# Making the 24 later value tiles between the residual MLP jobs, and spreading the gathers over the query/key jobs

## The chip, the cores and the metric

The kernel runs on one core of one Trainium2 chip, in one launch. The metric is device microseconds of one execution, the median of several runs. All data that passes between the stages lives in SBUF, PSUM or internal DRAM tensors of the core.

## The reference

Two transformer-like layers on x of 4 x 1024 x 128 (float32). Only layer 0 bears on the change:

```python
xn = layernorm(x)                                  # 4096 rows of 128
s  = attn(xn)     # 16 heads of 64: q, k, v = xn @ qkv_w.T; rope on q and k; softmax(q k / 8 + distance bias) v; @ out_w.T
a  = layer_norm(xn) * attn_nw + attn_nb
# top-1 of 8 experts, capacity 512 each, rows in order; a row beyond the capacity gets nothing from its expert
moe = combine(expert_mlp(dispatch(a)))             # 128 -> 512 -> 128, gelu
res = gelu(a @ res_inter_w + b) @ res_output_w + b # residual MLP
g  = silu(res * coef[:, :1] + moe * coef[:, 1:] + xn)
x  = x + s * g
```

Layer 1 follows (a recurrence and an MLP with LoRA experts); the change does not touch it.

## The kernel before

The program is a row of blocks. Every engine runs its own instruction list in a block, ordered by hand, and the engines meet only at semaphores; all of them meet at the end of a block. The blocks are `prepare`, `experts`, `project`, `attend`, `recur` and `finish`. In `prepare` and `experts` all loops are unrolled; the 64 jobs of `project` and the 64 head units of `attend` run in hardware loops (`Fori`).

`prepare` (0 to 168 us of the span) loads x, normalizes it, transposes it to `xn_t` and `a_t`, and computes the routing logits. The rows are 32 tiles of 128 rows. The value projection of one tile, `xn_t` (128 columns) times `wv` (128 x 1024), is two halves of 512 columns. Each half is one float32 matmul into PSUM (recorded as two passes), a ScalarE copy to bfloat16 (the high part), a subtraction PSUM minus high part (the low part), and each finished tile is written to DRAM (`vscr`, 512 KB) for the attention. The first 8 tiles (NV) are made here, between the transposes (L317 to L326, L381 to L390). The routing then goes as a long chain of small VectorE operations (L272 to L313) with one visit to TensorE for counts (L375, L376, at `COUNT_JOB = 1`). Its last result is `scatter_idx`, on which GpSimd waits to issue 32 indirect scatters, one for each tile, of the rows of A into `dispatch` (L235).

Beside this chain TensorE and ScalarE run the residual MLP in 8 jobs of 512 rows: `hidden(j)`, four matmuls of 128x512 (L351), a gelu of each on ScalarE (L410) into one of two buffers, `out(j)`, 16 matmuls of 128x128 (L363), and a copy of the result into G0 (L161). TensorE's order is `hidden(j+1)`, then `out(j)`.

`experts` (169 to 238 us) runs the 8 expert MLPs and makes the rope tables. `project` (238 to 552 us) first makes the other 24 value tiles, in the same way, in 8 PSUM half slots and four SBUF buffers, with SP issuing the writes (L701). Meanwhile GpSimd issues 32 indirect gathers of expert rows (L720), waits for all, multiplies them by the combine weight (L724) and adds them to G0 (L726) in two operations over the whole 128 x 4096 array; ScalarE then applies silu to G0 (L764). Only then do the query/key jobs start, 64 of them (8 head pairs of 8 chunks of 512 rows). A job is four float32 matmuls (L798), three VectorE operations on 128x1024 for rope (L665, L666, L670), a ScalarE copy to bfloat16 (L678), a GpSimd subtraction for the low part (L684), and a write of 512 KB from ScalarE's queue (L689). Two PSUM buffers, two to four SBUF buffers in a ring; VectorE may be three jobs ahead of GpSimd (`lo_ready`), and the write trails the copy by two jobs (`LEAD`).

Of the kernel before, what the change touches and what calls it, by code (L numbers as in the profile page):

```python
# [100 lines left out]
def prepare(nc, K, io, sb, ps, sem):  # L101
# [31 lines left out]
    lps, counts = ps("logit_ps", [P, NT, E + 2]), ps("count_ps", [P, 2, NT, E])  # L133
# [8 lines left out]
    va_wr = [sem(f"va_wr{s}") for s in range(2)]  # L142

# [10 lines left out]
    COUNT_JOB = 1  # L154

    def hidden_ps(i):
        return tp[i // 2][:, i % 2 * CH:i % 2 * CH + CH]
# [9 lines left out]
    with nc.Block() as block:  # L167
# [72 lines left out]
        def _(v):  # L240
# [31 lines left out]
            ch.link(v.tensor_copy(lg[:], lps[:]))  # L272
# [40 lines left out]
            v.tensor_copy(scatter_idx[:], col[:, 11, :]).then_inc(idx_ready, 1)  # L313

        @block.tensor
        def _(pe):
            def v_rows(t):  # L317

                pe.wait_ge(K.wv_in, DMA)
                pe.wait_ge(tr_out, 2 * (t // BT) + 1)  # L320
                for c in range(2):
                    if t >= 1:
                        pe.wait_ge(va_taken, 2 * t + c - 1)
                    pe.matmul(op[c][:].rearrange("p t d -> p (t d)"), K.XNT[:, t * P:t * P + P],
                              K.wv[:, c * CH:c * CH + CH], start=True, stop=True).then_inc(va_ready, 1)
# [21 lines left out]
            def hidden(j):  # L347
                for i in range(FT):
                    if j >= 1:
                        pe.wait_ge(h_out, FT * (j - 1) + i + 1)  # L350
                    pe.matmul(hidden_ps(i), w1r[:, i * P:i * P + P], AT[:, j * CH:j * CH + CH],  # L351
                              start=True, stop=True).then_inc(h_ready, 1)

            def out(j):
                s = j % 2
                if j >= 2:
                    pe.wait_ge(o_out, j - 1)
                else:
                    pe.wait_ge(va_taken, 2 * NV)
                for i in range(FT):  # L360
                    pe.wait_ge(h_out, FT * j + i + 1)
                    for c in range(CT):
                        mm = pe.matmul(op[s][:, c, :], hT[s][:, i, c * P:c * P + P], w2r[:, i, :],  # L363
                                       start=(i == 0 and c == 0), stop=(i == FT - 1), skip_group_check=True)
                mm.then_inc(o_ready, 1)

            hidden(0)
            for j in range(NR):
                if j + 1 < NR:
                    hidden(j + 1)  # L370
# [6 lines left out]
                out(j)  # L377

        @block.scalar
        def _(act):  # L380
# [23 lines left out]
            act.wait_ge(va_lo, 2 * NV)  # L404
            for j in range(NR):
                for i in range(FT):
                    act.wait_ge(h_ready, FT * j + i + 1)
                    if j >= 2 and i == 0:
                        act.wait_ge(o_ready, j - 1)
                    act.activation(hT[j % 2][:, i, :], hidden_ps(i), ACT.Gelu_apprx_tanh,  # L410
                                   bias=b1r[:, i:i + 1]).then_inc(h_out, 1)
                if j >= 1:
                    take_out(act, j - 1)
            take_out(act, NR - 1)
# [13 lines left out]
def experts(nc, K, io, sb, ps, sem):  # L428
# [30 lines left out]
    with nc.Block() as block:  # L459

        @block.sync
        def _(sp):
# [3 lines left out]
            for i in range(P // (DH // 2)):  # L466
                sp.dma_start(freq[32 * i:32 * i + 32, :], io["freqs"].rearrange("(p o) -> p o", o=1)).then_inc(fr_in, DMA)
            sp.dma_start(bp[:], io["bias_p"]).then_inc(bp_in, DMA)
# [151 lines left out]
def project(nc, K, io, sb, ps, sem):  # L620

    v_ready, vhi, vlo, v_wr = sem("v_ready"), sem("vhi"), sem("vlo"), [sem(f"v_wr{s}") for s in range(4)]
    wqk_in = [sem("wqk_in0"), sem("wqk_in1")]
# [5 lines left out]
    wv = K.wv  # L629
    NW = NT - NV  # L630
    vt = [sb(f"v_parts{i}", [P, H, 2, DH], BF16) for i in range(4)]
    wqk = [sb(f"wqk{i}", [P, 4, P]) for i in range(2)]
# [59 lines left out]
    with nc.Block() as block:  # L692

        @block.sync
        def _(sp):
            for r in range(2):
                sp.dma_start(wqk[r][:], io["wqk"][r]).then_inc(wqk_in[r], DMA)
            for t in range(NW):
                sp.wait_ge(vhi, 2 * t + 2)
                sp.wait_ge(vlo, 2 * t + 2)  # L700
                sp.dma_start(K.vscr[NV + t], vt[t % 4][:].rearrange("p h a d -> p h (a d)")).then_inc(v_wr[t % 4], DMA)  # L701
            for s in range(4):
                sp.wait_ge(v_wr[s], DMA * NW // 4)
# [12 lines left out]
        @block.gpsimd  # L716
        def _(g):

            for t in range(NT):
# [12 lines left out]
        @block.vector  # L732
        def _(v):
            for t in range(NW):
                for c in range(2):
                    n = 2 * t + c
                    v.wait_ge(vhi, n + 1)
                    hs = slice(c * H // 2, c * H // 2 + H // 2)
                    v.tensor_tensor(vt[t % 4][:, hs, 1, :],
                                    pp[n // 4 % 2][:, n % 4, :].rearrange("p (h d) -> p h d", d=DH),  # L740
                                    vt[t % 4][:, hs, 0, :], ALU.subtract).then_inc(vlo, 1)

            v.wait_ge(vlo, 2 * NW)
# [9 lines left out]
        def _(act):  # L753
            for t in range(NW):
                if t >= 4:
                    act.wait_ge(v_wr[t % 4], DMA * (t // 4))
                for c in range(2):
                    n = 2 * t + c
                    act.wait_ge(v_ready, n + 1)
                    act.copy(vt[t % 4][:, c * H // 2:c * H // 2 + H // 2, 0, :],  # L760
                             pp[n // 4 % 2][:, n % 4, :].rearrange("p (h d) -> p h d", d=DH)).then_inc(vhi, 1)

            act.wait_ge(mix_ready, 1)
            act.activation(K.G0[:], K.G0[:], ACT.Silu).then_inc(g0_ready, 1)  # L764

# [9 lines left out]
            run_jobs(act, step)  # L775
            for s in range(4):
                act.wait_ge(qk_wr[s], G * (DMA * NJ // 4) + 1)

        @block.tensor
        def _(pe):  # L780
            for t in range(NW):
                for c in range(2):
                    n = 2 * t + c
                    if n >= 8:
                        pe.wait_ge(vlo, n - 7)
                    pe.matmul(pp[n // 4 % 2][:, n % 4, :], XNT[:, (NV + t) * P:(NV + t + 1) * P], wv[:, c * CH:c * CH + CH],
                              start=True, stop=True).then_inc(v_ready, 1)
# [795 lines left out]
def program(nc, io):  # L1583

    with ExitStack() as outer:
# [27 lines left out]
        with ExitStack() as heads:  # L1613
# [5 lines left out]
            with ExitStack() as layer0:  # L1619
                sb0, _ = maker(layer0)  # L1620
                K.XNT = sb0("xn_t", [P, B * S])
                K.wv, K.wv_in = sb0("wv", [P, H * DH]), sem("wv_in")
                K.COS, K.SIN = sb0("cos_tables", [P, 2, S]), sb0("sin_tables", [P, 2, S])
# [72 lines left out]
```

## Time and profile before

| | us |
|---|---|
| median of 3 runs (2015.58 to 2019.97) | 2019.54 |
| the profiled execution, its own time | 2019.78 |
| its span, first to last instruction | 2018.0 |
| busy: TensorE, VectorE, GpSimd, ScalarE | 1810.2, 1517.4, 1470.0, 1149.4 |
| mean granted TensorE clock, share of full speed | 0.956 |

The span is read from the first to the last instruction of the core; 1.8 us of the profiled execution's time lie around it. An engine's busy time over the whole span is an average over blocks with different limits, so the change has to be judged block by block. The page's chain of work that ended last reaches back only over some 3% of the span, inside the last block, and does not reach the blocks of the change.

### The profile page before, as it was taken

The numbers are of one execution on the slowest core, as the hardware profiler recorded it, in microseconds if no ns is written. First come the engines' busy times: TensorE is split into PE (matmuls) and PEld (weight loads), VectorE is DVE, ScalarE is ACT, GpSimd is POOL, SyncE is SP. The second block draws the span as 40 slices with busy tenths as digits, with TensorE's granted clock in tenths as the row PEclk, the third lists the DMA queues.
The fourth block names the chain that finished last, engine by engine and source line by source line (L and its number), as shares of the span: only waits on it lengthen the run. The fifth ranks groups of instructions, "written<-read, shape, count | busy, mean of one in ns | idle before, by whom it ended". The sixth has DMA issues, their size and how long they took to land. (4 is left out here: it accounts for less than half of the span.)

```text
span 2018.0 us, 39811 instructions
## 1 busy us (share of the span) xinstructions
PE 1810.2 (90%) x12166; PEld 1052.0 (52%) x12356; DVE 1517.4 (75%) x2940; ACT 1149.4 (57%) x1691; POOL 1470.0 (73%) x865
## 2 busy tenths in 40 slices
PE   3959879999779999999999989999999999599978
PEld 2636523333245555555555555555555555356656
DVE  8303548999888888878878888878888888698841
ACT  3413533222267777777777767777777777322123
POOL 4260274555579999989989899899899899655521
PEclk8779979999989999999999999999999999799989
DMA  4212483446569888888888888888888888500001
GB/s 138 94 42 62 127 203 128 151 146 210 167 135 180 185 194 178 193 185 180 193 180 183 186 177 184 188 182 182 187 183 184 197 184 184 135 1 1 1 6 37
DMA packets 714150, 295.28 MB, mean 146 GB/s; under 512 B 619264, under 2 KB 678658, under 8 KB 714064
## 3 DMA queue, kind: packets, MB, share of 16 engines
q1 hardware_dynamic: 678240, 257.81, 56.5%
q10 hardware_dynamic: 33792, 33.56, 4.9%
q0 software_dynamic: 2048, 3.15, 1.2%
q8 instruction: 23, 0.38, 0.1%
q14 instruction: 47, 0.39, 0.1%
HBM read 102.39 MB, written 58.85 MB: 80 GB/s over the span
## 5 line engine op out<-in xcount | busy, mean ns | idle before, releaser
L1134 POOL TENSOR_TENSOR probs_lo<-probs 128x1024 bf16<-128x1024 f32 x512 | 957.1, 1901 | 78.9 <-DMA probs_t_lo<-probs_lo 51.3
L1102 ACT ACTIVATE probs<-scores,neg_max 128x1024 f32<-128x1024 f32 x512 | 588.6, 1150 | 264.0 <-DVE neg_max L1028 232.6
L1028 DVE CUSTOM_DVE_ANT_0 scores<-score_ps,bias_tab 128x1024 f32<-128x1024 f32 x512 | 624.8, 1221 | 116.9 <-issue 111.6
L952 PE MATMUL score_ps<-k_lo_lo,q_hi_lo 128*128 128x512 bf16 x1024 | 392.8, 384 | 35.8 <-DVE ident_bf L1088 15.6
L960 PEld LDWEIGHTS turn_ps<-ident_bf,probs 128*128 128x128 bf16 x4096 | 273.2, 98 | 144.6 <-issue 25.3
L960 PE MATMUL turn_ps<-ident_bf,probs 128*128 128x128 bf16 x4096 | 314.9, 220 | 18.9 <-ACT probs L1102 18.8
L951 PE MATMUL score_ps<-k_hi_hi,q_hi_lo 128*128 128x512 bf16 x834 | 321.4, 385 | 2.1 <-DMA k_lo_lo<-qk_parts 2.1
L979 PE MATMUL pv_ps<-probs_t_hi,v_hi_lo 128*128 128x512 bf16 x1024 | 262.9, 380 | 10.4 <-DVE share L1068 7.0
L1109 ACT COPY probs_t_hi<-turn_ps 128x1024 bf16<-128x1024 bf16 x256 | 255.9, 1000 | 21.2 <-PE turn_ps L960 17.3
L798 PE MATMUL proj_ps<-xn_t,wqk 128*128 128x512 f32 x512 | 231.1, 604 | 7.2 <-DVE rotated L670 5.8
L684 POOL TENSOR_TENSOR qk_parts<-rotated,qk_parts 128x1024 bf16<-128x1024 f32 x64 | 136.3, 2132 | 111.0 <-ACT qk_parts L678 110.8
L951 PEld LDWEIGHTS score_ps<-k_hi_hi,q_hi_lo 128*128 128x128 bf16 x1024 | 100.8, 98 | 168.8 <-DVE neg_max L1028 44.5
L1050 DVE COPY probs_t_hi<-turn_ps 128x1024 bf16<-128x1024 bf16 x256 | 175.6, 686 | 0.0
L1142 POOL TENSOR_TENSOR s<-s,share 128x512 f32 (+1 forms) x128 | 163.7, 1279 | 6.9 <-DVE share L1068 6.9
L798 PEld LDWEIGHTS proj_ps<-xn_t,wqk 128*128 128x128 f32 x512 | 92.1, 189 | 146.3 <-issue 92.3
L678 ACT CAST qk_parts<-rotated 128x1024 bf16<-128x1024 f32 x64 | 66.9, 1046 | 170.6 <-DVE rotated L670 161.7
L952 PEld LDWEIGHTS score_ps<-k_lo_lo,q_hi_lo 128*128 128x128 bf16 x1024 | 101.2, 99 | 92.0 <-issue 3.0
L1350 POOL TENSOR_TENSOR q_state<-state,q_t 128x1024 f32<-128x1024 f32 x32 | 76.5, 2391 | 81.8 <-DVE state L1294 72.5
L984 PE MATMUL pv_ps<-probs_t_lo,v_hi_lo 128*64 128x512 bf16 x1024 | 134.7, 385 | 0.0
L979 PEld LDWEIGHTS pv_ps<-probs_t_hi,v_hi_lo 128*128 128x128 bf16 x1024 | 87.4, 98 | 81.1 <-DVE share L1068 19.5
L1102 ACT ACTIVATION_READ_ACCUMULATOR probs<-scores,neg_max 128x1 f32 x512 | 96.1, 188 | 0.0
L997 PE MATMUL pv_ps<-wo_parts,out_t_hi 128*128 (+1 forms) x512 | 92.7, 224 | 2.8 <-DVE out_t_lo L1058 2.8
(213 smaller groups left out, 2392.6 us busy)
## 6 DMA issues: line engine op xcount, KB each, us to landing
qk_parts<-qk_parts ACTq DMA_DIRECT2D x64, 512.0 KB, 3.2
q_hi_lo<-qk_parts SPq DMA_DIRECT2D x128, 128.0 KB, 2.8
k_hi_hi<-qk_parts SPq DMA_DIRECT2D x128, 128.0 KB, 2.9
k_lo_lo<-qk_parts SPq DMA_DIRECT2D x128, 128.0 KB, 3.0
v_hi_lo<-v_parts SPq DMA_DIRECT2D x64, 256.0 KB, 3.2
bias_tab<-bias_by_distance SPq DMA_DIRECT2D x16, 960.0 KB, 6.2
v_parts<-v_parts SPq DMA_DIRECT2D x24, 512.0 KB
probs_t_lo<-probs_lo SPq DMA_TRANSPOSE x512, 3.3
```

What stands on the lines that cost most here:

```text
L684: g.tensor_tensor(parts[s][:, 1::2, :], rq[s][:], parts[s][:, 0::2, :], ALU.subtract).then_inc(lo_ready, 1)
L798: mm = pe.matmul(pp[s][:, i, :], wqk[r][:, i, :], rows, start=True, stop=True)
L951: pe.matmul(o[:, cs[c]], QS[s][:, q], KS[s][:, cs[c]], start=True, stop=False)
L952: mm = pe.matmul(o[:, cs[c]], QS[s][:, q], KL[s][:, cs[c]], start=False, stop=True)
L960: mm = pe.transpose(tp[n % 2][:, k, :], PRB[n % NP][:, k * P:k * P + P], ident16[:])
L979: mm = pe.matmul(ov[i][:], VV[h][:, k, :], PT[:, r:r + 4, k, :], start=(k == 0), stop=False, skip_group_check=True)
L1028: v.tensor_tensor_reduce(SB[n % 2][:], sp_[n % 2][:], TB[s][:, j:j + S], -1.0, 3.0e38, ALU.add, ALU.min, neg_max[:, n % 16:n % 16 + 1]).th ...
L1050: v.tensor_copy(PT[:, n % U, :, :], tp[n % 2][:]).then_inc(hi_dve, 1)
L1102: act.activation(PR[n % NP][:], SB[n % 2][:], ACT.Exp, bias=neg_max[:, m:m + 1], scale=-1.0, accum_out=row_sum[:, m:m + 1]).then_inc(exped, 1)
L1109: act.copy(PT[:, n % U, :, :], tp[n % 2][:]).then_inc(hi_act, 1)
L1134: g.tensor_tensor(LQ[n % NL][:], PR[n % NP][:], PRB[n % NP], ALU.subtract).then_inc(low_made, 1)
L1142: g.tensor_tensor(acc, acc, SH[c][:], ALU.add).then_inc(added, 1)
```

## The change

1. `prepare`: after `COUNT_JOB`, the 24 later value tiles are made, four for each residual job 1 to 6. The four of job 1 stand together after `out(1)`, and the first waits for `scatter_idx` (`idx_ready`), since the PSUM bank of the counts and that of the logits now serve as the two half slots. In jobs 2 to 6 one tile stands after every second of the four `hidden` steps and one after every second of the four `out` steps, on TensorE and correspondingly on ScalarE. There is one PSUM slot for each half instead of four. The high and low parts go to four buffers that share the space of the rope tables (`K.COS`, `K.SIN`), which are made later. ScalarE issues the 24 writes; VectorE makes the 48 low parts after it has finished the routing.
2. `project`: the value tiles and their writes are gone. GpSimd's loop is unrolled: after each low part of jobs 0 to 47 it issues a gather in two jobs out of three (32 in all); in jobs 48 to 62 after every second low part stands one of 8 smaller mixture operations (multiply or add, each over 128x1024). The silu of G0 moves to the end of ScalarE's list, behind the last write's issue.
3. The first two loads of `wqk` move from `project` to `experts`, into SP's list of small loads.

```diff
+    vb_ps = [logit_bank[:].rearrange("p (h d) -> p h d", d=DH),
+             counts[:].rearrange("p a t e -> p (a t e)").rearrange("p (h d) -> p h d", d=DH)]
+    W_JOBS = 6
+    def late_tile(j, k):
+        return 4 * (j - COUNT_JOB) + k if COUNT_JOB <= j < COUNT_JOB + W_JOBS else None
...
+            for t in range(NW):
+                for c in range(2):
+                    v.wait_ge(vb_hi, 2 * t + c + 1)
+                    v.tensor_tensor(vw[t % 4][:, v_heads(c), 1, :], vb_ps[c], vw[t % 4][:, v_heads(c), 0, :],
+                                    ALU.subtract).then_inc(vb_lo, 1)
...
+            def late(t):
+                if t is None:
+                    return
+                for c in range(2):
+                    if t >= 1:
+                        pe.wait_ge(vb_lo, 2 * t + c - 1)
+                    elif c == 0:
+                        pe.wait_ge(idx_ready, 1)
+                    pe.matmul(vb_ps[c].rearrange("p h d -> p (h d)"), K.XNT[:, (NV + t) * P:(NV + t + 1) * P],
+                              K.wv[:, c * CH:c * CH + CH], start=True, stop=True).then_inc(vb_ready, 1)
+            for j in range(NR):
+                for i in range(FT):
+                    if j + 1 < NR:
+                        hidden(j + 1, i)
+                    if i % 2 and j != COUNT_JOB:
+                        late(late_tile(j, i // 2))
...
+                for i in range(FT):
+                    out(j, i)
+                    if i % 2 and j != COUNT_JOB:
+                        late(late_tile(j, 2 + i // 2))
+                if j == COUNT_JOB:
+                    for k in range(4):
+                        late(late_tile(j, k))
...
+            def late_write(t):
+                act.wait_ge(vb_lo, 2 * t + 2)
+                act.dma_start(K.vscr[NV + t], vw[t % 4].rearrange("p h a d -> p h (a d)")).then_inc(vb_wr[t % 4], DMA)
+            def late_high(t):
+                if t is None:
+                    return
+                if t >= 4:
+                    act.wait_ge(vb_wr[t % 4], DMA * (t // 4))
+                for c in range(2):
+                    act.wait_ge(vb_ready, 2 * t + c + 1)
+                    act.copy(vw[t % 4][:, v_heads(c), 0, :], vb_ps[c]).then_inc(vb_hi, 1)
+                if t >= 2:
+                    late_write(t - 2)
...
-            g.wait_ge(gath, DMA * NT)
-            g.tensor_tensor(K.MOE[:], K.MOE[:], last_axis(K.coef_moe[:], D), ALU.mult).then_inc(mixed, 1)
-            g.wait_ge(mixed, 1)
-            g.tensor_tensor(K.G0[:], K.G0[:], K.MOE[:], ALU.add).then_inc(mix_ready, 1)
-            with g.Fori(0, G) as gi:
+            for gi in range(G):
                 for j, b, c in jobs():
                     lo_part(g, gi, j)
+                    n = gi * NJ + j
+                    if n < 3 * NT // 2:
+                        if n % 3 < 2:
+                            gather(n // 3 * 2 + n % 3)
+                    elif n % 2 == 0:
+                        k = (n - 3 * NT // 2) // 2
+                        if k == 0:
+                            g.wait_ge(gath, DMA * NT)
+                        (mix, mix_in)[k % 2](k // 2)
...
             run_jobs(act, step)
+            act.wait_ge(mix_ready, B)
+            act.activation(K.G0[:], K.G0[:], ACT.Silu).then_inc(g0_ready, 1)
```

## Rows read from the trace of the kernel before

**Rows 1.** Windows by stage: length, busy us of each engine (x instructions), PEclk, DMA share, GB/s.
```profile
101.00:117.00 16.00, 16.00 (x94) 11.70 (x93) 0.00 (x0) 4.71 (x7) 11.98 (x13) 1.00 0.13 43
117.00:147.00 30.00, 6.20 (x20) 4.62 (x20) 0.00 (x0) 2.20 (x4) 19.43 (x20) 0.58 0.13 36
147.00:169.00 22.00, 21.07 (x117) 15.45 (x118) 0.00 (x0) 8.83 (x14) 0.09 (x1) 0.87 0.06 17
...
252.00:285.00 33.00, 18.76 (x32) 5.87 (x30) 6.95 (x11) 5.93 (x11) 21.98 (x22) 0.70 0.81 136
...
305.00:549.00 244.00, 231.12 (x512) 92.07 (x512) 226.32 (x193) 71.13 (x66) 136.35 (x64) 0.99 0.47 158
```

**Rows 2.** Timeline, ScalarE, first stage: start us, us, line, operation, [idle before <-releaser].
```profile
134.13 0.59 ACT L161 COPY g<-res_out_ps 128x512 f32<-128x512 f32 x1 [24.43 <-remote]
139.75 0.69 ACT L410 ACTIVATE res_hidden_t<-prep_t,b_res_cols 128x512 f32<-128x512 f32 x1 [5.03 <-remote]
...
168.03 0.59 ACT L161 COPY g<-res_out_ps 128x512 f32<-128x512 f32 x1 [2.99 <-PE res_out_ps L363]
```

**Rows 3.** Groups by line from 117 to 147 us: busy us, mean ns, idle before <-releaser.
```profile
L235 POOL DMA_INDIRECT dispatch<-s,scatter_idx x20 | 19.5, 974 | 6.1 <-issue 6.1
L363 PE MATMUL res_out_ps<-w_res,res_hidden_t 128*128 128x128 f32 x20 | 6.7, 356 | 23.8 <-issue 23.8
```

**Rows 4.** Groups by line up to 380 us: value tiles, gathers, expert mixture.
```profile
L739 DVE TENSOR_TENSOR v_parts<-proj_ps,v_parts 128x512 bf16<-128x512 f32 x48 | 32.6, 691 | 36.0 <-ACT v_parts L760 17.6 <-issue 17.1
L720 POOL DMA_INDIRECT moe_rows<-expert_rows,gather_idx x32 | 32.0, 1000 | 76.4 <-POOLq L459 66.9 <-issue 9.4
...
L726 POOL TENSOR_TENSOR g<-g,moe_rows 128x4096 f32<-128x4096 f32 x1 | 8.8, 8841 | 0.1
...
L724 POOL TENSOR_TENSOR moe_rows<-moe_rows,coef_moe 128x4096 f32<-128x4096 f32 x1 | 7.0, 7038 | 5.2 <-DMA moe_rows<-expert_rows,gather_idx 5.2
```

**Rows 5.** Timeline, third block, its start.
```profile
238.29 18.15 PE L786 MATMUL proj_ps<-wv,xn_t 128*128 128x512 f32 x38 [6.99 <-PEq L459]
...
240.38 0.59 ACT L760 CAST v_parts<-proj_ps 128x512 bf16<-128x512 f32 x1 [6.51 <-PE proj_ps L786]
```

**Rows 6.** Timeline, third block, end of the value tiles and first query/key job.
```profile
301.18 0.59 ACT L760 CAST v_parts<-proj_ps 128x512 bf16<-128x512 f32 x1 [0.33 <-PE proj_ps L786]
...
302.90 0.59 ACT L760 CAST v_parts<-proj_ps 128x512 bf16<-128x512 f32 x1 [0.33 <-PE proj_ps L786]
...
305.13 7.14 PE L798 MATMUL proj_ps<-xn_t,wqk 128*128 128x512 f32 x16 [1.46 <-DVEq L745]
305.60 3.62 ACT L764 ACTIVATE g<-g 128x4096 f32<-128x4096 f32 x1
...
308.87 1.23 DVE L665 TENSOR_TENSOR proj_ps<-proj_ps,sin_tables 128x1024 f32<-128x1024 f32 x1 [3.85 <-PE proj_ps L798]
```

**Rows 7.** Timeline, first stage, around the end of the routing.
```profile
98.58 0.59 ACT L161 COPY g<-res_out_ps 128x512 f32<-128x512 f32 x1 [3.75 <-PE res_out_ps L363]
...
100.23 0.18 DVE L313 CAST scatter_idx<-route_cols 128x32 uint32<-128x32 f32 x1
...
101.36 1.22 POOL L235 DMA_INDIRECT dispatch<-s,scatter_idx  x1 [20.07 <-issue]
...
105.58 0.59 ACT L161 COPY g<-res_out_ps 128x512 f32<-128x512 f32 x1 [2.88 <-issue]
```

**Rows 8.** Timeline, end of the query/key jobs and start of the attention block.
```profile
545.69 3.81 ACTq L689 DMA_DIRECT2D qk_parts<-qk_parts  x3
546.81 2.12 POOL L684 TENSOR_TENSOR qk_parts<-rotated,qk_parts 128x1024 bf16<-128x1024 f32 x1 [1.40 <-ACT qk_parts L678]
...
552.66 1.28 ACT L1102 ACT_TABLE_LOAD   x1 [5.93 <-PEq L692]
```

**Rows 9.** Groups by line in the query/key jobs, 305 to 548 us.
```profile
L684 POOL TENSOR_TENSOR qk_parts<-rotated,qk_parts 128x1024 bf16<-128x1024 f32 x64 | 136.3, 2132 | 111.0 <-ACT qk_parts L678 110.8
...
L665 DVE TENSOR_TENSOR proj_ps<-proj_ps,sin_tables 128x1024 f32<-128x1024 f32 x64 | 78.7, 1229 | 12.2 <-PE proj_ps L798 12.2
```

More of the change, by code:

```diff
@@ L142, in prepare @@
     va_wr = [sem(f"va_wr{s}") for s in range(2)]
+    NW = NT - NV
+    vw = [(K.COS, K.SIN)[i // 2][:, i % 2, :].bitcast(BF16).rearrange("p (h a d) -> p h a d", a=2, d=DH) for i in range(4)]
+    vb_ready, vb_hi, vb_lo, vb_wr = sem("vb_ready"), sem("vb_hi"), sem("vb_lo"), [sem(f"vb_wr{s}") for s in range(4)]
+    vb_ps = [logit_bank[:].rearrange("p (h d) -> p h d", d=DH),
+             counts[:].rearrange("p a t e -> p (a t e)").rearrange("p (h d) -> p h d", d=DH)]
     def v_tiles(n):
@@ L345, in _ @@
             pe.wait_ge(res_in, 2 * DMA)
-            def hidden(j):
-                for i in range(FT):
[L349 to L370, printed above, removed]
+            def hidden(j, i):
+                if j >= 1:
+                    pe.wait_ge(h_out, FT * (j - 1) + i + 1)
+                pe.matmul(hidden_ps(i), w1r[:, i * P:i * P + P], AT[:, j * CH:j * CH + CH],
+                          start=True, stop=True).then_inc(h_ready, 1)
+            def out(j, i):
+                s = j % 2
+                if j >= 2 and i == 0:
+                    pe.wait_ge(o_out, j - 1)
+                elif i == 0:
+                    pe.wait_ge(va_taken, 2 * NV)
+                pe.wait_ge(h_out, FT * j + i + 1)
+                for c in range(CT):
+                    mm = pe.matmul(op[s][:, c, :], hT[s][:, i, c * P:c * P + P], w2r[:, i, :],
+                                   start=(i == 0 and c == 0), stop=(i == FT - 1), skip_group_check=True)
+                if i == FT - 1:
+                    mm.then_inc(o_ready, 1)
@@ L371, in _ @@
+            for i in range(FT):
+                hidden(0, i)
+            for j in range(NR):
+                for i in range(FT):
+                    if j + 1 < NR:
+                        hidden(j + 1, i)
+                    if i % 2 and j != COUNT_JOB:
+                        late(late_tile(j, i // 2))
                 if j == COUNT_JOB:
@@ L404, in _, with gelu @@
             act.wait_ge(va_lo, 2 * NV)
+            def gelu(j, i):
+                act.wait_ge(h_ready, FT * j + i + 1)
+                if j >= 2 and i == 0:
+                    act.wait_ge(o_ready, j - 1)
+                act.activation(hT[j % 2][:, i, :], hidden_ps(i), ACT.Gelu_apprx_tanh,
+                               bias=b1r[:, i:i + 1]).then_inc(h_out, 1)
+            def late_write(t):
[11 more added lines that the diff above has]
+                    late_write(t - 2)
+            for i in range(FT):
+                gelu(0, i)
             for j in range(NR):
                 for i in range(FT):
[L407 to L414, printed above, removed]
+                    if j + 1 < NR:
+                        gelu(j + 1, i)
+                    if i % 2 and j != COUNT_JOB:
+                        late_high(late_tile(j, i // 2))
+                if j == COUNT_JOB:
+                    take_out(act, j)
+                    for k in range(4):
+                        late_high(late_tile(j, k))
+                else:
+                    late_high(late_tile(j, 2))
+                    take_out(act, j)
+                    late_high(late_tile(j, 3))
+                    if late_tile(j, 3) == NW - 1:
+                        late_write(NW - 2)
+                        late_write(NW - 1)
+            for s in range(4):
+                act.wait_ge(vb_wr[s], DMA * NW // 4)
 def load_expert(sp, K, io, e):
@@ L467, in _ @@
                 sp.dma_start(freq[32 * i:32 * i + 32, :], io["freqs"].rearrange("(p o) -> p o", o=1)).then_inc(fr_in, DMA)
+            for r in range(2):
+                sp.dma_start(K.wqk[r][:], io["wqk"][r]).then_inc(K.wqk_in[r], DMA)
             sp.dma_start(bp[:], io["bias_p"]).then_inc(bp_in, DMA)
@@ L620, in project @@
 def project(nc, K, io, sb, ps, sem):
-    v_ready, vhi, vlo, v_wr = sem("v_ready"), sem("vhi"), sem("vlo"), [sem(f"v_wr{s}") for s in range(4)]
-    wqk_in = [sem("wqk_in0"), sem("wqk_in1")]
     qk_ready, pair, turned = sem("qk_ready"), sem("pair"), sem("rope_turned")
@@ L628, in project @@
     COS, SIN = K.COS, K.SIN
[L629 to L632, printed above, removed]
+    wqk, wqk_in = K.wqk, K.wqk_in
     t1 = [sb(f"rope_cos{i}", [P, 2, CH]) for i in range(2)]
@@ L695, in _ @@
         def _(sp):
[L696 to L703, printed above, removed]
             with sp.Fori(0, G // 2 - 1) as gh:
@@ L717, in _, with gather @@
         def _(g):
-            for t in range(NT):
+            def gather(t):
                 g.indirect_dma_start(out=K.MOE[:, t, :], out_offset=None, in_=K.eout,
@@ L753, in _ @@
         def _(act):
[L754 to L764, printed above, removed]
             for s in range(4):
@@ L780, in _ @@
         def _(pe):
[L781 to L787, printed above, removed]
             with pe.Fori(0, G // 2) as gh:
@@ L1622, in program @@
                 K.wv, K.wv_in = sb0("wv", [P, H * DH]), sem("wv_in")
+                K.wqk, K.wqk_in = [sb0(f"wqk{i}", [P, 4, P]) for i in range(2)], [sem(f"wqk_in{i}") for i in range(2)]
                 K.COS, K.SIN = sb0("cos_tables", [P, 2, S]), sb0("sin_tables", [P, 2, S])
```

22 lines of the change are left out of this document (10 added, 12 removed).

## The prediction

> **What bounds the kernel now.** I read the windows by stage first, then the timeline of the stages that the change touches, then the groups by line in them. The windows [rows 1] show where an engine is full. In the query/key jobs (305 to 549 us) TensorE is busy for 231 of 244 us and VectorE for 226, so this stretch is bound by work. In the first stage the picture breaks in two. From 101 to 117 us TensorE is busy throughout. From 117 to 147 us it does 6.2 us of work in 30, with 20 matmuls and 20 weight loads, and from 147 us it is full again. The same happens in the third block from 252 to 285 us: 18.8 us of work in 33.
>
> Nothing in those two stretches has too much to do. ScalarE makes one copy at 134.13 us after 24.43 us of idling that the view puts down to "remote", that is to no instruction of the profile, and the next gelu waits another 5.03 us in the same way [rows 2]. TensorE's 20 matmuls have 23.8 us of idle ahead of them, all "issue" [rows 3]: its instructions come one by one, 30 us for 40 of them, 0.75 us each. What both stretches share is GpSimd issuing indirect DMAs, 20 of them in the first [rows 3], 32 from the block's start in the second [rows 4], with the slowness setting in some 14 us after their start. I call this the slow stretch, and the forecast hangs on how it treats the moved work. A transfer as a cause is not read directly: in 117 to 147 us the DMA share is only 0.13 [rows 1].
>
> **The third block loses the value tiles.** It starts them at 238.29 us [rows 5] and the first query/key matmul comes at 305.13 us [rows 6]: 66.8 us go. Once it flows, a tile of two halves takes 1.72 us (301.18 to 302.90 [rows 6]), so 24 need 41.3 us, and 25.5 us of the 66.8 are slow stretch. The jobs then start on a TensorE that has just been idle: its first value half took 2.1 us to the ScalarE copy (238.29 to 240.38 [rows 5]) against 0.86 for a later one, so I add 1.4 us for the first job's four matmuls. Gain: 65.4 us.
>
> **The first stage takes them in.** Up to `scatter_idx` (written by 100.4 us [rows 7]) nothing changes. TensorE ends `out(1)` at about 98.5 us and then waits until 100.6 for the first late tile, with all later residual jobs queued behind that wait. Without any slow stretch it would go on so:
> - Four tiles in a row, each half having one PSUM slot: matmul 0.86, copy 0.59 [rows 6], subtraction 0.69 [rows 4] and three hand-overs at an assumed 0.15 make 2.6 us for a tile: 10.4 us.
> - Five jobs (2 to 6). A job alone took 7.0 us (98.58 to 105.58 [rows 7]), plus four tiles at 1.72: 13.9 us each, 69.5 us. Between two tiles stand two hidden or eight small out matmuls, about 1.7 us, which covers the copy and subtraction of the tile before. ScalarE has four gelus at 0.69 [rows 2], nine copies at 0.59 and four DMA issues, at most 1.27 us each (3.81 for three [rows 8]): 13.2 us, just under TensorE's.
> - The last `out`, its copy and the switch of blocks: 5.3 us.
>
> That is 85.2 us of work from 100.6 us, to 185.8 us, against 168.9 us before (last copy 168.03 to 168.62 [rows 2], and the switch). +16.9 us is the lower bound: TensorE was idle for most of the slow stretch, and if all of that idle could be used, the 41 us of tiles would cost only this.
>
> I do not believe it can. What is slow is the arrival of instructions, and the late tiles are instructions: 4 for each half on TensorE, one each on ScalarE and VectorE. The scatters stay where they are, so the stretch should end at 147 us again. Starting at about 115 us (between ScalarE's 109.7, which is 134.13 less 24.43 [rows 2], and TensorE's 117), 14.4 us of the 85.2 are done before it. During it 32 us at 0.75 give TensorE 43 instructions; a late job has 112 for its 13.9 us, so 5.3 us of progress; ScalarE's four operations in 30 us [rows 1] against 13 for a job give 4.3. I take 4. Left at 147: 66.8 us, end at 213.8, +44.9 us. The upper bound has ScalarE stop at 109.7 with nothing done in the stretch: 76.1 us left, +54 us. I stay near 45, since both engines' records lie there.
>
> The 24 writes go from SP's queue to ScalarE's, behind a wait for a tile two back, already subtracted; a buffer comes back after four tiles, 7 us or more. The last one has `out(7)` of 3.6 us as cover. VectorE is idle here after the routing. All of this I cost at nothing; uncovered, the last write would cost at most its landing, about 3 us.
>
> **Gathers in the jobs.** GpSimd's low part takes 2.13 us of a 3.7 us job and it idles 111 us over the 64 [rows 9]. A gather is 1.0 us [rows 4] and repeats every 1.3 (1.28 in the scatters: 19.5 and 6.1 us over 20 [rows 3]). 2.13 + 1.3 = 3.43 is under 3.7, and two jobs in three have one. A mixture operation is a fourth of 7.04 or 8.84 us [rows 4], at most 2.2; with it a pair of jobs needs 6.5 of 7.4 us, and VectorE may be three jobs ahead. So GpSimd stays hidden. What a gather does to the others is the open price. Before, 32 gathers at 1.3 us spacing went with 25.5 us lost, 0.8 us each. Now there is one in 5.5 us, the slowness needed some 14 us of dense issue to set in, and the other engines run loops. I take 0, bounds 0 and 25 us.
>
> A rule speaks against that 0: the Trainium skill, "DMA: Bandwidth & Descriptors", section "SWDGE vs HWDGE vs iDMA", says that gathers from GpSimd and transfers issued by SP or ScalarE sit in different queues of the same DMA engines, which take turns between them. By it the jobs' 512 KB writes would be held up by each gather even at this spacing. The rule alone gives no size; no row of the jobs holds a gather.
>
> **The end of the third block.** The last low part (546.81 us [rows 8]) now stands behind the last mixture addition, which starts at about 545.4 and takes 2.2 us: +0.8. Silu, before at 305.60 with nobody waiting [rows 6], now follows the last write's issue at 549.5 us: table load 1.28 [rows 8] and 3.62 [rows 6] end at 554.4, plus 0.8, against a block end of about 551.8 before. +3.4 us, bounds 0 and 5. The moved `wqk` loads are 2 issues behind loads that matter later: 0.
>
> **Sum.** -65.4 + 44.9 + 0 + 3.4 = -17.1 us. Against the profiled execution's 2019.8 us (span 2018.0) that is 2002.7; its time stands 0.2 us over the median, so the median comes to about 2002.5. I say 2003.
>
> **The rivals.**
> 1. *The slow stretch does not touch the late tiles.* They fill TensorE's idle and the first stage costs +16.9: sum -45, 1975 us. For it: TensorE is idle 24 of those 30 us. Against it: ScalarE's 24.43 us without a releaser. Chance 0.12. The Trainium skill ("Runtime: NRT & Kernel Launch", "Instruction fetch mechanics") says that the next block of instructions is fetched while the current one runs, so crossings are mostly hidden; by it there would be no slow stretch from fetching and the end would be this rival's. The trace disagrees where indirect DMAs run [rows 2, 3].
> 2. *Slower: gathers keep their price in the jobs.* Each costs the other engines 0.8 us wherever it stands: +25 us, sum +8, 2028 us. It decides from 0.53 us for each gather (17.1 / 32). For it: both slow stretches go with indirect DMAs. Against it: TensorE and VectorE ran undisturbed through the first 11 gathers. Chance 0.15.
> 3. *The single PSUM slot sets the pace.* Every late tile takes 2.6 us, as the four in a row, instead of 1.72: 20 x 0.9 = 18, 2021 us, no change. It needs ScalarE to be late, which it nearly is at 13.2 of 13.9. Chance 0.10.
>
> **How the numbers follow.** My forecast has 0.60, with a range of its own of 1993 to 2014 us (first stage +35 to +54, end 0 to 5). The other 0.03 are mixtures of 2 and 3, slower. A measurement here tells 0.2%, 4 us, from no change. Faster: 0.60 + 0.12 and a third of rival 2 at a smaller price, 0.77. Same: most of rival 3, 0.08. Slower: 0.15. The range reaches toward rivals 1 and 2 and leaves out their far ends, 0.1 each: 1980 to 2024 us.
>
> **What would show it.** In the profile after, `experts` should start at about 214 us instead of 168.9, still with ScalarE waits of many us without a releaser between 110 and 147, now ahead of late copies; no value matmul in the third block; its first job right at its start and jobs still 3.7 us apart; GpSimd's low parts without waits of VectorE on them; attention starting 3 to 4 us later after the last rope operation than now. I am wrong if `experts` starts before 200 (rival 1), if jobs 0 to 47 take longer than jobs 48 to 63 (rival 2), or if late tiles after 147 us come more than 3.6 us apart on average (rival 3).

## The result, and the profile after

The changed kernel takes 2001.15 us (median of 4 runs, 1998.13 to 2003.84); the kernel before, run beside it, 2017.56 us (4 runs, 2013.66 to 2019.97). The ratio is 0.9896, 95% interval 0.9872 to 0.992: faster by some 1%. The profiled execution took 1998.13 us, its span 1996.4 us against 2018.0.

Windows of the changed kernel (length, busy us of each engine with its instructions, granted clock, DMA share, GB/s, as in [rows 1]):

```profile
101.00:117.00 16.00, 14.95 (x30) 5.31 (x30) 6.92 (x10) 8.60 (x14) 12.34 (x13) 0.92 0.37 140
117.00:147.00 30.00, 8.72 (x39) 6.07 (x37) 1.38 (x2) 1.77 (x4) 18.86 (x20) 0.68 0.19 59
147.00:169.00 22.00, 21.24 (x69) 11.43 (x70) 8.48 (x13) 12.19 (x21) 0.00 (x0) 0.90 0.39 153
169.00:190.00 21.00, 21.00 (x89) 12.49 (x88) 8.49 (x13) 11.92 (x20) 0.00 (x0) 1.00 0.38 151
...
292.00:536.00 244.00, 224.02 (x497) 89.12 (x496) 222.97 (x190) 72.32 (x67) 184.98 (x104) 0.98 0.51 167
```

The second line answers to the second of [rows 1]: the slow stretch lies at the same place, 39 matmuls and four ScalarE operations in 30 us. The late tiles did not fill it; they were caught in it. The timeline of ScalarE in the first stage shows the same, and the pace behind it:

```profile
122.33 0.58 ACT L459 CAST cos_tables<-count_ps 128x512 bf16<-128x512 f32 x1 [2.89 <-issue]
...
146.40 0.58 ACT L459 CAST sin_tables<-logit_ps 128x512 bf16<-128x512 f32 x1 [23.48 <-remote]
...
163.76 0.58 ACT L172 COPY g<-res_out_ps 128x512 f32<-128x512 f32 x1 [1.20 <-PE res_out_ps L377]
177.63 0.58 ACT L172 COPY g<-res_out_ps 128x512 f32<-128x512 f32 x1 [1.20 <-PE res_out_ps L377]
191.51 0.58 ACT L172 COPY g<-res_out_ps 128x512 f32<-128x512 f32 x1 [1.20 <-PE res_out_ps L377]
205.38 0.58 ACT L172 COPY g<-res_out_ps 128x512 f32<-128x512 f32 x1 [1.20 <-PE res_out_ps L377]
```

The copy after 23.48 us without a releaser is now a late tile's high part (L459), 12 us later than the residual copy of [rows 2]. Four copies of residual results (L172) stand 13.87 us apart, so a late job takes what was forecast (13.9). The timeline of the block starts and of the end of the third block (answers to [rows 5, 6, 8]):

```profile
212.90 1.93 PE L573 MATMUL dt_ps<-ident,dispatched 128*128 128x128 f32 x8 [2.26 <-PEq L178]
...
282.13 8.32 PE L843 MATMUL proj_ps<-xn_t,wqk 128*128 128x512 f32 x12 [7.34 <-DVEq L807]
288.77 1.23 DVE L731 TENSOR_TENSOR proj_ps<-proj_ps,sin_tables 128x1024 f32<-128x1024 f32 x1 [8.77 <-PE proj_ps L843]
...
524.34 1.22 DVE L736 TENSOR_TENSOR rotated<-proj_ps,rope_cos 128x1024 f32<-128x1024 f32 x1
525.28 2.35 POOL L789 TENSOR_TENSOR g<-g,moe_rows 128x1024 f32<-128x1024 f32 x1
527.58 2.13 POOL L750 TENSOR_TENSOR qk_parts<-rotated,qk_parts 128x1024 bf16<-128x1024 f32 x1
530.31 1.28 ACT L827 ACT_TABLE_LOAD   x1 [3.67 <-POOL qk_parts L750]
531.61 3.62 ACT L827 ACTIVATE g<-g 128x4096 f32<-128x4096 f32 x1
535.49 1.28 ACT L1147 ACT_TABLE_LOAD   x1 [0.27 <-PEq L758]
```

At the end the chain is easy to read: the last low part stands behind the last mixture addition, the write's issue and the table load behind the low part, then silu, then the block ends. Groups by line in the jobs (answers to [rows 9]):

```profile
L750 POOL TENSOR_TENSOR qk_parts<-rotated,qk_parts 128x1024 bf16<-128x1024 f32 x64 | 136.1, 2129 | 123.9 <-ACT qk_parts L744 122.6 <-issue 0.7
L778 POOL DMA_INDIRECT moe_rows<-expert_rows,gather_idx x32 | 32.6, 1019 | 4.8 <-issue 2.6
L789 POOL TENSOR_TENSOR g<-g,moe_rows 128x1024 f32<-128x1024 f32 x4 | 9.4, 2360 | 0.0
L784 POOL TENSOR_TENSOR moe_rows<-moe_rows,coef_moe 128x1024 f32<-128x1024 f32 x4 | 7.6, 1901 | 0.0
```

### The profile page after: what moved, and what is told of

Read it like the earlier page. It is cut to its first block and busy times, and to the rows that moved or that the text cites. A ratio compares the mean times of both kernels' runs of the same rounds, so it can differ in the third digit from the quotient of the medians.

```text
span 1996.4 us, 39713 instructions
## 1 busy us (share of the span) xinstructions
PE 1798.6 (90%) x12166; PEld 1046.5 (52%) x12356; DVE 1516.6 (76%) x2940; ACT 1149.6 (58%) x1691; POOL 1472.0 (74%) x871
## 5 line engine op out<-in xcount | busy, mean ns | idle before, releaser
L1154 ACT COPY probs_t_hi<-turn_ps 128x1024 bf16<-128x1024 bf16 x256 | 255.7, 999 | 21.2 <-PE turn_ps L1005 17.0
```

What stands on the lines that cost most here:

```text
L1154: act.copy(PT[:, n % U, :, :], tp[n % 2][:]).then_inc(hi_act, 1)
```

## The experiments

They ran on four chips, here called B to E; each was compared with the kernel before on its own chip (B 2022.95 us, 7 runs; C 1996.98, 7 runs; D 2000.86, one run; E 1997.44, 11 runs). The first comparison's chip is not named in its record. That the kernel before differs by 26 us between chips turned out to be part of the answer. Where no range is given, a time is of a single run.

**The spreading alone** (chip B): the kernel before, its value tiles left in the third block, with the gathers and mixture spread as in the change, silu at the end.

```diff
-            g.tensor_tensor(K.MOE[:], K.MOE[:], last_axis(K.coef_moe[:], D), ALU.mult).then_inc(mixed, 1)
-            g.wait_ge(mixed, 1)
-            g.tensor_tensor(K.G0[:], K.G0[:], K.MOE[:], ALU.add).then_inc(mix_ready, 1)
...
+            for gi in range(G):
                 for j, b, c in jobs():
                     lo_part(g, gi, j)
+                    n = gi * NJ + j
+                    if n < 3 * NT // 2:
+                        if n % 3 < 2:
+                            gather(n // 3 * 2 + n % 3)
...
```

> The kernel before with the gathers and the expert mixture spread over the query/key jobs and silu at the end; the value tiles stay in the third block. Theory (dense indirect DMAs cause the slow stretch, spread ones do not): the 24 value tiles take 41 to 43 us instead of 66.8, the end of the block costs 3 us more as in the changed kernel, total about 1995 us, so at least as fast as the changed kernel, whose value move then would be worth nothing or less. Rival (moving the value tiles is what pays, the slow stretch of the third block has another cause): value tiles again take 60 us or more and the time stays at 2017 to 2021 us.

Measured: 2002.56 us (1999.83 to 2007.28), ratio 0.9898 (0.9882 to 0.9915). This is as large as the effect of the change in the first comparison (0.9896), without its largest part. TensorE's timeline in its third block:

```profile
236.97 44.17 PE L799 MATMUL proj_ps<-wv,xn_t 128*128 128x512 f32 x96 [7.00 <-PEq L459]
282.60 7.14 PE L811 MATMUL proj_ps<-xn_t,wqk 128*128 128x512 f32 x16 [1.46 <-DVEq L759]
```

45.6 us from the first value matmul to the first job, against 66.8 in the profile of before [rows 5, 6], which was taken in the first comparison: without gathers beside them the tiles run through. The mixture moved with the gathers, but before the change it started only at 285.65 us, after the slow part, so it is not what slowed the tiles.

**Pacing the scatters** (chip B): the changed kernel, each scatter waiting for late tiles, so that the 32 go out over 63 us (about 2.0 us apart) instead of every 1.28 us.

```diff
             for t in range(NT):
+                if t:
+                    g.wait_ge(vb_lo, 5 * t // 4)
                 g.indirect_dma_start(out=K.disp, out_offset=bass.IndirectOffsetOnAxis(scatter_idx[:, t:t + 1], 0),
...
```

> The changed kernel with each scatter held until the late value halves have come on (scatter t waits for 5t/4 of the 48 low parts), some 2.2 us apart instead of 1.28. Theory (the density of indirect DMAs makes the slow stretch): no wait of many us between 110 and 150 us, second block starts near 186 us instead of 213, total 1972 to 1978 us. Rival (each scatter costs the other engines a fixed 0.8 us or so, however spaced): no gain, 1998 to 2004 us. In between, if 2.2 us is still too dense.

Measured: 1972.55 us (1969.58 to 1983.33), ratio 0.9772 (0.974 to 0.9804). Its window and the start of its second block:

```profile
117.00:147.00 30.00, 30.00 (x131) 18.28 (x130) 12.35 (x18) 16.62 (x27) 13.51 (x14) 1.00 0.44 171
```
```profile
185.38 1.06 PE L575 MATMUL dt_ps<-ident,dispatched 128*128 128x128 f32 x8 [2.26 <-PEq L178]
```

The stretch is gone: TensorE full, clock 1.00, `experts` at 185.4, where the working without a slow stretch had put it (185.8).

**No scatters** (chip B): the 32 scatters left out, and SP's wait for them with them; the experts read zero rows.

```diff
-            sp.wait_ge(scat, DMA * NT)
+            sp.wait_ge(zero_out, 4 * DMA)
...
-            for t in range(NT):
-                g.indirect_dma_start(out=K.disp, out_offset=bass.IndirectOffsetOnAxis(scatter_idx[:, t:t + 1], 0),
...
```

> The changed kernel with the 32 scatters left out, so that the experts get rows of zeros. Theory: without indirect DMAs there is no slow stretch, TensorE works through, second block starts at 185 to 187 us (the 185.8 that I worked out for no slow stretch), total about 1973 us. Rival (the slow stretch has another cause, such as the writes or the order of the late tiles): second block still starts after 205 us.

Measured: 1977.07 us; TensorE 30.00 of 30 us busy from 117 to 147, `experts` at 185.9. Without dense scatters there is no stretch on this chip, and pacing them does as much as leaving them out.

**Every row in bounds** (chip B): row i is scattered to place i, so none is dropped; the experts get other rows than the reference's.

```diff
+            g.iota(scatter_idx[:], pattern=[[P, NT]], base=0, channel_multiplier=1).then_inc(pool_own, 1)
+            g.wait_ge(pool_own, 3)
...
-            v.tensor_copy(scatter_idx[:], col[:, 11, :]).then_inc(idx_ready, 1)
+            v.nop().then_inc(idx_ready, 1)
```

> The changed kernel with another destination for each scattered row: row i goes to place i, so that no row is dropped and no place is used twice (the experts get other rows than in the reference). Theory (density of issue is what matters): slow stretch as in the changed kernel, second block starts at 210 to 215 us. Rival (the rows that are dropped for lack of capacity, more and more of them in the later tiles, make the stretch): no slow stretch, second block starts near 186 us.

Measured: 2000.29 us, `experts` at 214.2, TensorE 5.94 us busy from 117 to 147, ScalarE waiting 27.59 us without a releaser. Dropped rows are not the cause.

**Dense gathers beside the looped jobs** (chips C and D): all 32 gathers and the mixture at the block's start as before, the jobs running; to free them of GpSimd, ScalarE writes the high part twice in place of the low part, so the attention gets other numbers.

```diff
         act.copy(parts[s][:, 0::2, :], rq[s][:]).then_inc(hi_ready, 1)
+        act.copy(parts[s][:, 1::2, :], rq[s][:]).then_inc(lo_ready, 1)
...
-            for gi in range(G):
-                for j, b, c in jobs():
-                    lo_part(g, gi, j)
...
+            for t in range(NT):
+                gather(t)
+            g.wait_ge(gath, DMA * NT)
```

> The changed kernel with the 32 gathers issued densely at the start of the third block, while the query/key jobs run: ScalarE writes the high part a second time in place of GpSimd's low part, which is left out, so that the jobs do not need GpSimd. Theory (the slow stretch is a slow arrival of instructions in unrolled lists; hardware loops are immune): jobs 3.7 us apart from the first on, also during the 42 us of gathers. Rival (dense indirect DMAs slow whatever runs beside them, by transfers or by semaphores): from about 14 us after the first gather until 5 us after the last the jobs come 6 us or more apart, or ScalarE waits for writes, some 20 us lost in all.

> As dense_in_loops, to be read beside the control of this call. If the control shows slow stretches: theory (only unrolled lists suffer) has the jobs 3.7 us apart through the gathers; rival (whatever runs beside dense indirect DMAs) has them 6 us or more apart from about 14 us on. If the control shows none in the first stage, it says this for the gathers alone, and only if the control's value tiles are slow.

Measured: 1975.16 us on C, 1976.51 on D. Its window on chip C:

```profile
270.00:302.00 32.00, 31.25 (x70) 12.46 (x69) 30.61 (x27) 15.19 (x16) 21.42 (x22) 1.00 0.86 146
```

With 22 gathers in 32 us, TensorE and VectorE are full. From the first rope operation to the last are 235.57 us (262.09 to 497.66), the same as in the changed kernel, and 235.56 on chip D (260.77 to 496.33). But this window also held the first surprise: on chip C the first stage had no slow stretch either, with dense scatters (TensorE 30.00 of 30 us). So this run does not tell whether hardware loops protect the jobs on a chip that has the stretch.

**Value tiles moved, gathers left dense** (chip C): the other half of the change, alone.

```diff
+            for t in range(NT):
+                gather(t)
+            g.wait_ge(gath, DMA * NT)
...
+            with g.Fori(0, G) as gi:
                 for j, b, c in jobs():
                     lo_part(g, gi, j)
```

> The value tiles moved as in the changed kernel, but the 32 gathers and the mixture as one piece ahead of GpSimd's low parts, as before. GpSimd starts its first low part some 42 + 5 + 17 = 64 us after the block's start, VectorE can be three jobs ahead, about 11 to 14 us, so the jobs stand still for about 50 us: total 2045 to 2055 us. If it is under 2020 us, the spreading was not needed for the move.

Measured: 2019.05 us, 22 above this chip's kernel before. VectorE's timeline names the wait:

```profile
319.39 1.22 DVE L736 TENSOR_TENSOR rotated<-proj_ps,rope_cos 128x1024 f32<-128x1024 f32 x1 [40.25 <-POOL qk_parts L750]
```

With no value tiles in front, the jobs stand behind the gathers and the mixture on GpSimd's list for 40 us, where some 50 were expected. The expected 2045 to 2055 was for a chip with the stretch.

**Two bursts of 16 scatters** (chip C), to see how long dense issue may last.

```diff
+                if t == 16:
+                    g.wait_ge(vb_lo, 24)
```

> The changed kernel with the scatters in two dense bursts of 16, the second after half of the late value halves. If something fills up over about 11 to 13 dense indirect DMAs and drains in a pause, each burst has a short slow stretch of 5 to 8 us at its end, and the second block starts at 190 to 202 us. If dense issue from the first DMA on were the cause, however short, it would start at 213 us as in the changed kernel; if only very long bursts matter, at 186.

Measured: 1972.66 us, no stretch. On this chip 32 in a row give none either, so it says nothing.

**Paced, with an earlier silu** (chip C): one gather in each of the first 32 jobs, the mixture in the next 16, silu ahead of the last 8 jobs.

```diff
-                    if n < 3 * NT // 2:
-                        if n % 3 < 2:
-                            gather(n // 3 * 2 + n % 3)
...
+                    if n < NT:
+                        gather(n)
...
+                if isinstance(gi, int) and gi == G - 1 and u == 0:
+                    act.wait_ge(mix_ready, B)
+                    act.activation(K.G0[:], K.G0[:], ACT.Silu).then_inc(g0_ready, 1)
```

> The paced kernel with a gather after each of the first 32 jobs, the 8 mixture operations after every second job of 32 to 46, and silu after job 56's write instead of the last. Theory (silu behind the last write costs the block's end about 3 us, and earlier it is hidden by the jobs' slack): the attention block starts some 3 us earlier after the last rope operation than in the paced kernel, 1967 to 1971 us. Rival (GpSimd or ScalarE in the jobs becomes the bound when it carries more in fewer jobs): jobs 0 to 31 or 56 to 63 more than 3.7 us apart, 1973 us or more.

Measured: 1973.33 us (1970.58 to 1977.91), ratio 0.9896 (0.9866 to 0.9926). From the start of the last rope operation to the attention are 8.25 us (496.90 to 505.15) against 11.15 in the paced kernel (496.34 to 507.49): the 2.9 us of the end are recovered, but 0.15% is too little for this comparison to show in the total. The ratio is also no lower than that of the change unpaced, 0.9896 in the first comparison and 0.9888 on chip E below: where there is no stretch, no gain from pacing shows.

**The kernel before once more** (chip D), to see whether the stretch belongs to the kernel.

> The kernel before, unchanged, as a control on the chip of this call, since on the chip of the last call it took 1997 instead of 2018 to 2023 us and none of the four kernels there had a slow stretch in the first stage. If this chip is like the first: 2015 to 2025 us, second block at 169 us, value tiles of the third block in 66 us. If it is like the other: 1990 to 2000 us, second block near 147 us; and if the value tiles then still take about 66 us beside the gathers, that slow stretch has a cause of its own; if about 43 us, both have the same, which that chip lacks, and 22 us more would have to be lost elsewhere.

Measured: 1990.59 us, 10.3 below the other run of the same kernel on this chip; single totals say no more than that here, so the reading goes by the trace. Its windows:

```profile
117.00:147.00 30.00, 21.14 (x141) 17.05 (x140) 0.00 (x0) 7.84 (x12) 20.52 (x22) 0.89 0.14 38
```
```profile
241.00:263.00 22.00, 15.76 (x33) 6.20 (x32) 6.62 (x11) 5.37 (x10) 12.91 (x13) 0.92 1.02 173
```

In the first stage the stretch is absent: TensorE finishes its list and `experts` starts at 146.15 us instead of 168.93, after an 8.86 us wait for the scattered rows. Yet the third block is as long as before, 62.3 us from first value matmul to first job (215.45 to 277.76). The waits of that block say why; first this run (215 to 278 us), then the trace of before (238 to 305 us), each from the first value matmul to the first job:

```profile
DVE v_parts L739 <- ACT v_parts L760: 31.6, 24, 6.5
...
ACT v_parts L760 <- DMA v_parts<-v_parts: 26.4, 14, 6.8
```
```profile
PEld proj_ps L786 <- issue: 39.4, 81, 7.2
...
DVE v_parts L739 <- issue: 17.1, 12, 3.6
...
ACT v_parts L760 <- DMA v_parts<-v_parts: 0.8, 2, 0.6
```

Columns: engine, tile and line, releaser; total us, times, longest. On chip D ScalarE waits 26.4 us for the 512 KB writes to free their buffers, with the DMA share at 1.02 from 241 to 263 us; in the trace of before 0.8 us, and much of the time is in "issue". Two different limits cost the block nearly the same.

**The change and the spreading alone, on one chip more** (chip E), both kernels as they stand above.

> The changed kernel once more, beside the next one and the kernel before on one chip. What is open: whether the change's gain depends on the slow stretch of the first stage. If this chip shows the stretch, 2001 us again, with experts starting near 213. If it shows none, experts starts near 186, attention near 507 and the time is 1971 to 1976 us; the kernel before is then 1990 to 1997 and the ratio again near 0.99, because both kernels lose the same stretch. The rival says that late tiles lie in the slow stretch's idle time only where there is one, so the ratio would differ from 0.99 by more than 0.005 on a chip without it.

> The kernel before with only the gathers and the mixture spread over the jobs, value tiles left in the third block. Theory: moving the value tiles is worth nothing with or without a slow stretch, because TensorE is full in either place and a tile costs 1.72 us in both; so this kernel is within 4 us of the changed kernel run beside it, on whichever chip (about 2002 us where the stretch stands, about 1975 where it does not). The rival, that the moved value tiles carry part of the gain, expects it 8 to 20 us above the changed kernel on a chip without the stretch.

Measured: the change 1975.05 us (1973.46 to 1982.8), ratio 0.9888 (0.987 to 0.9905); the spreading alone 1978.58 us (1973.54 to 1987.68), ratio 0.9912 (0.9889 to 0.9935). No stretch in either (from 117 to 147 us TensorE is busy 30.00 of 30 us in the first; in the second 21.00, and it has then ended its list). The starts of the changed kernel's second and third block, then those of the other:

```profile
185.06 1.06 PE L573 MATMUL dt_ps<-ident,dispatched 128*128 128x128 f32 x8 [2.27 <-PEq L178]
...
254.47 9.36 PE L843 MATMUL proj_ps<-xn_t,wqk 128*128 128x512 f32 x16 [7.34 <-DVEq L807]
```
```profile
145.30 1.97 PE L502 MATMUL dt_ps<-ident,dispatched 128*128 128x128 f32 x8 [8.99 <-DMA dispatched<-dispatch]
...
214.54 42.84 PE L799 MATMUL proj_ps<-wv,xn_t 128*128 128x512 f32 x96 [7.00 <-PEq L459]
258.83 7.14 PE L811 MATMUL proj_ps<-xn_t,wqk 128*128 128x512 f32 x16 [1.46 <-DVEq L759]
```

The value tiles cost 39.8 us in the first stage (145.30 to 185.06) and 44.3 us in the third block (214.54 to 258.83). From there to the attention the changed kernel needs 252.7 us (254.47 to 507.15) and the other 250.5 (258.83 to 509.30), since its first job is slower; 2.2 us are left at the attention's start and 3.5 between the medians, where the two intervals overlap. Without the stretch, moving them is worth at most that. With it no pair was run on one chip: the attention starts at 535.49 us in the changed kernel and at 533.06 in the spreading alone on chip B, so no gain from the move shows there either.

## Why the prediction came out right, step by step

| term | forecast | profile before to after |
|---|---|---|
| first stage | +44.9 | +44.0 (168.93 to 212.90) |
| third block, first matmul to first rope operation | -65.4 | -63.9 (70.58 to 6.64) |
| jobs, first to last rope operation | 0 | 0.0 (235.56 to 235.57) |
| last rope operation to attention | +3.4 | +2.9 (8.23 to 11.15) |
| attention starts | -17.1 | -17.2 (552.66 to 535.49) |
| attention to the end of the span | 0 | -4.4 (1465.3 to 1460.9) |

The second block, not in the sum, took 0.1 us less. The errors of the terms (-0.9, +1.5, -0.5) cancel in part, so the hit to 0.1 us at the attention's start is better than the working deserves.

**First stage.** The forecast let the late tiles stand in the slow stretch for its whole length and resume at 147 us; they resumed at 146.4. The four tiles in a row took 2.6 us each (101.82, 104.58, 107.11, 109.63), the jobs 13.87. That the stretch depends on the scatters, assumed from their standing beside it, is now shown on chip B by two edits that remove it (pacing, leaving out); that the dropped rows do not make it, by a third.

The reason that the prediction gave, a slow arrival of instructions, is not shown, and the traces speak against one form of it. They record transfers on two queues of kind "instruction", q8 and q14. The queues of the changed kernel from 117 to 147 us (packets, MB, share), and TensorE's return:

```profile
q1 hardware_dynamic: 1685, 0.84, 9.9%
q0 software_dynamic: 672, 0.39, 5.1%
q10 hardware_dynamic: 146, 0.52, 4.4%
```
```profile
147.76 2.07 PE L390 MATMUL logit_ps<-wv,xn_t 128*128 128x512 f32 x2 [16.66 <-DVE sin_tables L328]
```

There is no instruction packet in the stretch, nor anywhere from 109 to 157 us, and yet ScalarE goes on at 146.40 and TensorE at 147.76: what let them go on was not the landing of such a packet. In the kernel before a packet of q8 lands between 111 and 113 us with the stretch and without it (chip D); the next follows at 133 to 136 us on chip D and only after 160 us in the first comparison, as if it waited for TensorE and not TensorE for it. The view does not say whether these two queues carry every engine's instructions. So the forecast was right that the stretch holds up whatever stands on the lists, which the 44.0 us show; what holds the engines up ("issue" and "remote") stays open.

**Rival 1** (no stretch for the late tiles) did not happen in this comparison, but its mechanism is real elsewhere: the runs on C to E end near its 1975 us. There the kernel before is faster too, so the gain stays near 1.1% (ratio 0.9888 on chip E). But the absolute time and the sign by which this rival was to be known (`experts` before 200 us; 185.06 on chip E) would have come out its way: the forecast's +44.9 us holds only where the stretch stands, as it did in the profile that it was read from. By the Trainium skill ("Runtime: NRT & Kernel Launch", "Instruction fetch mechanics") the next instructions are fetched while the current ones run. The traces of C to E agree (with late tiles TensorE is busy 30.00 of 30 us there). The prediction took the slow stretch as evidence against it; the packets above do not bear that out.

**Third block.** The size was right, the reading of it too narrow. I put 25.5 us of the 66.8 down to the slow stretch. Spreading the gathers alone recovered 21.2 of them on chip B, so the gathers beside the tiles were the cause, but chip D takes 62.3 us with the DMA engines full and ScalarE's waits put down to the writes. The Trainium skill's rule of queues that take turns at the same DMA engines ("DMA: Bandwidth & Descriptors", "SWDGE vs HWDGE vs iDMA") agrees with that trace: share 1.02, 26.4 us of waits for writes; the trace shows the full engines, not the turns. I had used it only against the jobs. The first job came out slower than forecast: from the block's first matmul to the first rope operation 6.64 us against 3.74 for a job behind the value tiles (305.13 to 308.87 [rows 6]), +2.9 where I took +1.4. TensorE had stood idle for 7.34 us ahead of it, and its granted clock from 282 to 286 us is 0.50 (1.2 GHz), against 1.00 from 305 to 309 us in the kernel before.

**Rival 2** (gathers keep their price in the jobs) is refuted for this spacing: the 64 jobs take the same 235.6 us with one gather in 5.5 us, and on chips C and D with one in 1.3. On C the writes still landed 7.2 us (median of the seven from 255 to 302 us) after their issue and the buffers covered it. Not tested is the dense case on a chip with the stretch.

**Rival 3** (one PSUM slot sets the pace) is refuted: 13.87 us for a job with four tiles; only the four tiles in a row took 2.6 us each.

**The end** was mis-sized by 0.5 us. **The last 4.4 us** of the span are in blocks that the change does not touch, and no part of the effect: with the same code behind it, the distance from attention to the end is 1460.3 us in the paced run, 1473.9 in the changed kernel's profile on chip E, 1472.5 in the spreading alone on B. The medians differ by 16.4 us, the attention's start by 17.2.

So the gain does not come from where the diff is largest. In the first comparison the tiles' 41 us of TensorE work went from one place where TensorE had no usable time to spare to another of the same kind. On chip E the first stage did have some, 8.99 us at its end in which TensorE waited for the scattered rows, and still the tiles cost it 39.8 us. What pays is that the gathers left the value tiles' stretch: by the attention's start the spreading alone is 19.6 us ahead (552.66 in the profile of before, 533.06 on chip B), the loss at the end already taken off.

## What to carry to other kernels

A gap in an engine's work is not free room until the profile says what holds the engine up; work moved into a gap with no releaser can be held up as well, as here. Split a change into its halves: here the spreading has nearly the whole gain, and the move costs 22 us alone and brings at most 3.5 beside the spreading, while together they look like one idea. When indirect DMAs go out back to back beside other work, try spacing them out first: on chip B one wait in the scatter loop took the ratio to 0.9772, some 1.2% beyond the 0.9896 of the 24 moved tiles in the first comparison. On chip C, which has no stretch, it brought nothing that shows. That unrolled lists suffer and loops do not is not shown.

## What was not expected of the hardware

- The slow stretch beside dense scatters (one per 1.28 us from GpSimd) is a matter of the chip or of its condition: it stands in all four traces of the first comparison and chip B that have dense scatters, and in none of the six on chips C, D and E, with the same scatter code. It costs the kernel before 22.8 us in the first stage (168.93 against 146.15). Why is open.
- The same 32 gathers lengthen the value tiles on both kinds of chip, by 21.2 us (66.8 against 45.6) and 18.0 us (62.3 against 44.3, chips D and E), on chips with the stretch in waits named "issue" (first comparison), on chip D through writes that land late.
- Scatters about 2.0 us apart, in groups of up to four at 1.28 us, gave no stretch on chip B.
